# Four opening loads issued by ScalarE's queue instead of the sync queue

## What is computed

```
h       = relu(x @ W1[id] + b1[id])                 # 512 -> 128
adapted = h @ W2[id] + b2[id]                       # 128 -> 512
normed  = layernorm(x + adapted) * gamma[id] + beta[id]
x1      = x + normed
out     = x1 + x1 @ W[id2] + b[id2]                 # 512 -> 512
```

## Time and profile before

| | |
|---|---|
| median of 3 runs | 309.87 us |
| the profiled execution | 310.4 us |
| its span | 308.6 us |
| TensorE busy (matmul) | 301.1 us, 98% of the span |
| VectorE, ScalarE, GpSimd busy | 225.7, 212.0, 225.7 us |
| moved by DMA | 65.1 MB, 211 GB/s in the mean |
| granted TensorE clock | full from the first stretch to the last |

### The profile page before, as it was taken

How to read it: one execution, slowest core, us unless ns; L and a number is a source line. 1 busy time by engine, 2 the same in 40 slices (tenths; PEclk the granted TensorE clock), 3 DMA queues, 4 the chain that set the end, 5 groups by cost and what they waited for, 6 DMA issues and landing times.

```text
span 308.6 us, 4770 instructions
## 1 busy us (share of the span) xinstructions
PE 301.1 (98%) x1406; PEld 242.4 (79%) x1406; DVE 225.7 (73%) x643; ACT 212.0 (69%) x382; POOL 225.7 (73%) x185
## 2 busy tenths in 40 slices
PE   8789999999999999999999999999999999999995
PEld 6335788888888888888888888888888888888884
DVE  0089968886969879596887969688795968889610
ACT  1139778885887859686696858968596874867431
POOL 0299966999599995999779995999959994631000
PEclk9999999999999999999999999999999999999999
DMA  6999994879766896878866897668867371111122
GB/s 184 331 374 365 363 288 162 226 229 324 227 165 190 254 271 198 221 206 250 261 172 209 218 314 244 133 194 264 292 183 208 133 276 34 70 68 70 70 102 102
DMA packets 40817, 65.13 MB, mean 211 GB/s; under 512 B 6101, under 2 KB 10197, under 8 KB 40790
## 3 DMA queue, kind: packets, MB, share of 16 engines
q1 hardware_dynamic: 40498, 64.29, 67.8%
q10 hardware_dynamic: 292, 0.52, 0.5%
HBM read 48.03 MB, written 16.78 MB: 210 GB/s over the span
## 4 chain that ended last, share of the span: by engine, by line
PE 90%; DVE 3%; DMA 2%; SPq 2%; issue 1%; POOL 0%; ACT 0%; DVEq 0%
PE out_ps L814 56%; PE down_ps L814 13%; PE h_ps L814 13%; PE turn_ps L876 9%; DMA xrow<-x_rows 2%; DVE y L520 1%; SPq L177 1%; DVE stats L525 1%; SPq L186 1%; DVE turn_ps L564 0%; DVE x1T_lo L571 0%; POOL xrow L723 0%; PE out_ps L876 0%; ACT out_sb L423 0%; SPq L209 0%
## 5 line engine op out<-in xcount | busy, mean ns | idle before, releaser
L814 PE MATMUL out_ps<-x1T_hi,w_hi 128*128 128x512 f32 x256 | 100.0, 391 | 0.0
L814 PE MATMUL out_ps<-x1T_hi,w_lo 128*128 128x512 f32 x256 | 99.7, 389 | 0.0
L723 POOL TENSOR_TENSOR xrow<-xrow,b_rows 128x512 f32<-128x512 f32 x64 | 82.3, 1292 | 11.9 <-DMA xrow<-x_rows 11.7
L814 PE MATMUL out_ps<-x1T_lo,w_hi 128*128 128x512 f32 x256 | 68.6, 390 | 0.0
L414 ACT ACTIVATE x1T_hi<-turn_ps,gamma_beta 128x512 fp32r<-128x512 f32 x62 | 41.9, 690 | 37.7 <-DVE turn_ps L564 37.7
L564 DVE SCALAR_TENSOR_TENSOR turn_ps<-turn_ps,gamma_beta,xT 128x512 f32<-128x512 f32 x62 | 44.0, 752 | 32.4 <-PE turn_ps L876 31.7
L405 ACT ACTIVATE y<-y,shift,rstd 128x512 f32<-128x512 f32 x64 | 52.0, 817 | 22.0 <-DVE shift L555 21.7
L728 POOL TENSOR_TENSOR xT_lo<-xT,xT_hi 128x512 fp32r<-128x512 f32 x48 | 62.2, 1296 | 1.5 <-ACT xT_hi L354 1.5
L520 DVE TENSOR_TENSOR y<-down_ps,xrow 128x512 f32<-128x512 f32 x64 | 43.7, 684 | 19.8 <-PE down_ps L814 18.8
L814 PEld LDWEIGHTS out_ps<-x1T_hi,w_hi 128*128 128x128 f32 x256 | 48.1, 188 | 10.2 <-ACT x1T_hi L414 0.2
L814 PEld LDWEIGHTS out_ps<-x1T_hi,w_lo 128*128 128x128 f32 x256 | 48.1, 188 | 9.9
(11 more groups left out here) (50 smaller groups left out, 359.6 us busy)
## 6 DMA issues: line engine op xcount, KB each, us to landing
out_cols<-out_sb SPq DMA_DIRECT2D x64, 256.0 KB, 2.8
xrow<-x_rows SPq DMA_DIRECT2D x30, 512.0 KB, 6.7
xT<-x_cols SPq DMA_DIRECT2D x28, 512.0 KB, 6.1
w<-w_all SPq DMA_DIRECT2D x8, 1024.0 KB, 7.6
w<-w_all SPq DMA_DIRECT2D x16, 256.0 KB, 5.2
b_rows<-b_all SPq DMA_DIRECT2D x7, 256.0 KB, 8.8
xT<-x_cols SPq DMA_DIRECT2D x6, 256.0 KB, 6.0
xrow<-x_rows SPq DMA_DIRECT2D x4, 256.0 KB, 6.7
```

The source lines that it names most:

```text
L723: nc.gpsimd.tensor_tensor(xrow[:, i % XR, :], xrow[:, i % XR, :], b2_rows[:, m % 2, :], ALU.add).then_inc(rowbias_done, 1)
L814: mm = nc.tensor.matmul(out, lhsT, rhs, start=first and n == 0, stop=last and n == len(terms) - 1)
```

## The change

Row tiles 0, 1 and 2 and column tile 5 leave the sync queue's order and are issued by ScalarE's queue, after `load_table()` and before `spread_b2()`. The order of everything else on both queues stays, and so do all semaphores.

```diff
+        def load_first_rows(engine, i):
+            engine.dma_start(xrow[:, i, :], x_rows[i * P:(i + 1) * P, :]).then_inc(first_rows_in[i], 16)
...
                 load_w2(0)
-                load_first_rows(0)
                 load_first_cols(sp, 4)
-                load_first_cols(sp, 5)
                 load_first_cols(sp, 6)
-                load_first_rows(1)
-                load_first_rows(2)
-                load_first_rows(3)
+                load_first_rows(sp, 3)
                 load_rows(4)
...
                 load_ids()
                 load_table()
+                load_first_rows(act, 0)
+                load_first_rows(act, 1)
+                load_first_rows(act, 2)
+                load_first_cols(act, 5)
                 spread_b2()
```

More of the change, by code:

```diff
@@ L259, in load_cols @@
                              .rearrange("(c p) n -> p c n", p=P)).then_inc(cols_in[i // 2 % (XC // 2)], 16)
-            def load_first_rows(i):
-                sp.dma_start(xrow[:, i, :], x_rows[i * P:(i + 1) * P, :]).then_inc(first_rows_in[i], 16)
             def load_rows(i):
```

## The result

The changed kernel takes 312.24 us in the median of 9 runs (310.38 to 313.46), the one before 309.72 us beside it (309.22 to 310.41). The recorded ratio is 1.0073, with a 95% interval of 1.0058 to 1.0088 (it need not equal the quotient of the medians, which is 1.0081): slower, by 2.5 us in the medians, and outside the range. The spread is part of the result: the kernel before stays within 1.2 us, the changed one covers 3.1.

A forecast was written before the change was run, and what follows sets the result against it. TensorE bounds the kernel, through when `up(8)` and the first transposes can start. Column tile 4 0.5 us later, less 0.28, gives +0.2 us, nothing from column tiles 8 and 9: median 310.1 us, range 308.9 to 311.5.

The forecast's parts named there:

- ScalarE issuing early: In the opening, its four loads compete with w1, which lands at worst 2.7 us later, at 8.3; no further cost.
- the sum: Whole-kernel total: +0.2 us from the engine chain, nothing from the wait for column tiles 8 and 9; counts as no change.
- Column tile 4 was put at 12.6: Landing that `up(4)` waits for: middle of 10.9 to 14.3 us, against 12.1 before, so 0.5 us later.
- slower rival: At `up(4)`: queues take turns, loads overtake column tile 4; landing at 13.5 to 14.3 costs 1.1 to 1.9 us; chance 0.34.
- the eighth load before: Row tile 1 on the sync queue, landing at 14.3 us; taken as column tile 4's latest landing, 2.2 us later.
- the faster rival: From 5.5 to 11 us the second queue fills the DMA gaps; gain 0.6 to 1.2 us; chance 0.27.
- the load wall: Landing of column tiles 8 and 9 at 24.0, which `up(8)` waits for; to gain between nothing and 1.2 us.
- Both signs of the faster rival: DMA at 300 GB/s or more from 5.5 to 11 us, and column tiles 8 and 9 landed before 23.4.
- d - 0.28: From the addition of tile 4 on: shift is column tile 4's landing delay d less 0.28 us gained on VectorE.

The follow-up runs named there:

- the late start: Kernel before, loads unchanged, `up(0)` also waits for column tile 3: 312.97 us against 309.94, ratio 1.0097; with 20 warm-ups instead of 10, 310.94 us.
- the profile with 20 warm-ups: Changed kernel with 20 warm-up products instead of 10: median 311.31 us, ratio 1.0047 to the kernel before; profiled execution 311.07 us.
- on one queue: Kernel before, all on the sync queue, row tiles 1, 2 and column tile 5 ahead of column tile 4: 313.96 us against 309.76, ratio 1.0131.
- column tile 2 and the filling: Kernel before with column tile 2 issued by ScalarE and eight products of ones between `up(3)` and `up(4)`: 312.00 us, ratio 1.0063.

## Why the prediction was wrong

**The step that failed** is the one on ScalarE issuing early: "At worst w1 lands 4 x 0.67 = 2.7 us later, at 8.3. The first four `up` and the b2 product then reach `up(4)` some 4.0 us after that ... It costs nothing beyond." The case was seen and the landing well sized (8.4). Its price, put at nothing, was wrong twice.

First, the clock was no term of the sum. After 3.07 us without work TensorE took 7.14 us from `up(0)` to `relu(0)` (8.47 to 15.61) instead of 4.60 (5.73 to 10.33): 2.54 us. The front table's full clock "from the first stretch" was also read too trustingly, since the view prints 1.00 where it has no record. The pace shows it: with ScalarE's loads behind w1 the warm-ups' weight loads follow one another every 0.21 us up to 4.0 us, where that record begins, and every 0.11 us after.

Second, I followed the lateness only to `up(4)` and not to `down(0)`, which also waits for `relu(0)`. Before, `relu(0)` ended at 11.02 and `down(0)` started at 12.71: 1.7 us of cover. Of 2.74 us of late w1 that leaves 1.1 us even at full clock, and of 2.74 + 2.54 = 5.28 us it leaves 3.6; the profile shows 3.64 (12.71 to 16.35). From there to the first transpose 0.55 us come back. `down(4)` is 3.31 us late (20.09 to 23.40), `down(6)`, behind VectorE's shorter backlog, 3.10 (22.21 to 25.31), and the first transpose 3.09 (27.48 to 30.57). The vanished wait for column tiles 8 and 9 gave the transposes nothing. The experiments with the loads left as they were show the two parts apart: 1.0 us for the late start at full clock, 2.0 for the clock. In the median of the changed kernel the clock is less, 0.9 to 1.1 us. The rest has two candidates at full clock, which the runs do not separate: 1.1 us at `down(0)` from w1 as late as above, and 0.7 us from the late column tiles in the profile with 20 warm-ups.

**Right or nearly so.** Column tile 4 was put at 12.6 and landed at 12.9. The slower rival's mechanism was there: all four of ScalarE's loads landed ahead of it, and at the higher pace it still came at 12.9, not at the 14.3 of the eighth load before. In the profile at half clock it did not matter, since TensorE came to it two microseconds later; at full clock it set the start of `up(4)`. The gaps of the DMA engines were filled, as the faster rival had it, and the load wall moved from 24.0 to 22.5, more than its bound of 1.2; the bound had counted idle time alone, while the transfers too became faster at nearly the same share (0.94 and 254 GB/s, then 1.03 and 367). Both signs of the faster rival came, and the kernel was slower: they told of the loads, not of when TensorE starts. GpSimd no longer waited for row tile 1, and `down(4)` instead of VectorE's backlog set the addition of tile 4. The d - 0.28 came out within 0.1 us in three profiles at full clock. The copy of b2 was not delayed by the issues.

**Wrong side or missing.** `up(8)` was to start within 0.6 us of 24.10 and started at 27.01. The slower rival had the right sign, and with the load of column tile 4 only a part of the cause. Its price lacked the clock: on one queue `up(4)` 1.6 us late cost 4.2 us.

The Trainium skill, "DMA: Bandwidth & Descriptors", section "Queues, rings and completion order", has the engines go round robin between queues. The trace agrees in that row tile 1, issued 0.13 us after w1 on the other queue, landed before it (8.0 and 8.4), and w1, issued 0.26 us after the first of ScalarE's loads, took 5.6 us with four beside it, and 4.0 with one (2.80 to 6.8). The section "Issuing engines are not separate DMA queues" says that spreading only saves issue time; here it also changed which load comes first, and w1's delay came of it. On the clock, "TensorE: Matmul & The Clock Gate", section "Part 1: The HAM clock gate", makes the granted clock depend on how busy the engine has been; the late start agrees, with a fall to 0.50 after 3.40 us of rest and 1.00 after 0.59.

**Open**: why kernels with ScalarE's loads behind w1 remain 0.8 to 1.2 us slower in the median, when two of the three profiled executions (310.35 and 309.81 us) were equal to or faster than before and the third (311.71) had issued w1 late; what starts the slow opening after a rest of 1.48 us and not after one of 1.55; and the three executions of 312.7 to 312.9 us with column tile 2 and the filling.

## What to carry to other kernels

Before a load is moved to another queue, ask which load it will run beside, and how early the second queue really gets to it: the one to protect is the first that the bounding engine waits for, and the wait should be followed through every consumer, not only the next. A standstill of TensorE early on can cost more than the lateness that it brings (3.0 us instead of 1.0 in the late start), since the work behind it may run at half clock; here warm-ups that reached to the first real product kept it at full clock. When a change widens the spread of the executions, compare their clocks before the loads, and the durations of the weight loads too, since the recorded clock may begin after the slow stretch.

## What had not been expected of the hardware

- ScalarE's queue issued loads while its table was loading: the first at 2.53 us, the table load from 2.46 to 3.74.
- One 256 KB load issued 0.27 us ahead of another, on the other queue, made that one take 4.0 instead of 2.8 us; four made it 5.6, and 4.7 in another execution.
- With the four loads on two queues and issued earlier, the DMA engines moved 367 GB/s from 5.5 to 8 us, against 254 before.
- After rests of 3.07, 3.40 and 4.38 us TensorE went on at, or fell to, half clock; after 2.31 and 2.71 us it held in the profiled executions. After rests of 1.48 and 1.55 us early in the opening it went on at half clock in one profile and at full clock in the other; in the first the record of the clock began only at 10.3 us.
